# Two cross-attention layers in split fp32: the bias token's value added from its probabilities on VectorE instead of a 65-row product per head

## The reference, cut to what matters

```
x: (8, 100, 512)   ctx: (8, 361, 512)   H = 16 heads, K = 128
x = L0(x, ctx)                       # one attention without heads, residual
for i in (1, 2):                     # two layers with heads
    h  = layer_norm(x)
    qh = h @ wq + bq;  kh = ctx @ wk + bk;  vh = ctx @ wv + bv      # per head
    kh = concat([kh, bias_k]);  vh = concat([vh, bias_v])          # one more token
    w  = softmax(qh kh^T / sqrt(K));  c = w vh
    x  = x + c @ wo + bo
x = x + gelu(layer_norm(x) @ w_fc1 + b_fc1) @ w_fc2 + b_fc2
```

## Time and profile before

| | |
|---|---|
| median of 3 runs | 1837.41 us (1834.67 to 1837.85) |
| profiled execution, first to last instruction | 1836.4 us |
| TensorE busy | 1812.6 us, 99% |
| VectorE / ScalarE / GpSimd busy | 1122.9 / 805.7 / 761.4 us |
| mean granted TensorE clock | 0.998 |
| a layer pass | 389 us (129 to 518 us) in the first, 368 us (518 to 886 us) in the second |

### The profile page before, as it was taken

The page is one execution under the profiler, slowest core; times in us unless marked ns, Lnnn a source line. Parts: engine busy times, 40 slices in busy tenths (PEclk is TensorE's granted clock), DMA queues, the critical chain, the costliest instruction groups (busy, mean ns, idle before and its releaser), DMA issues.

```text
span 1836.4 us, 30800 instructions
## 1 busy us (share of the span) xinstructions
PE 1812.6 (99%) x11572; PEld 1776.0 (97%) x11572; DVE 1122.9 (61%) x2588; ACT 805.7 (44%) x1868; POOL 761.4 (41%) x624
## 2 busy tenths in 40 slices
PE   8999999999999999999999999999999999999999
PEld 5889999999999999999999999999999999999999
DVE  3667656565575565566687655566666556555565
ACT  3634334434444444344475443434435434434454
POOL 2674252352251453531478145252245252353244
PEclk9999999999999999999999999999999999999999
DMA  8933221121020121210373111111012020111122
GB/s 249 238 115 92 63 64 31 46 64 35 24 72 23 41 66 34 64 36 18 117 221 94 30 47 58 35 58 36 30 52 60 24 64 30 47 58 41 39 96 85
DMA packets 73590, 123.80 MB, mean 67 GB/s; under 512 B 13888, under 2 KB 25536, under 8 KB 73444
## 3 DMA queue, kind: packets, MB, share of 16 engines
q1 hardware_dynamic: 71140, 117.64, 21.7%
q10 hardware_dynamic: 2304, 4.20, 0.7%
HBM read 119.20 MB, written 2.61 MB: 66 GB/s over the span
## 4 chain that ended last, share of the span: by engine, by line
PE 90%; DVE 5%; DMA 2%; ACT 1%; issue 1%; POOL 0%; SPq 0%; DVEq 0%; ACTq 0%
PE psum L602 27%; PE psum L604 27%; PE psum L603 27%; PE psum L898 3%; PE psum L636 2%; DMA ctx_rows_in<-ctx_dram 1%; DVE xT L1568 1%; DMA key_stage_late<-head_w_dram 1%; PE psum L773 1%; PE psum L864 1%; PE psum L791 1%; PE psum L615 1%; PE psum L611 1%; DMA key_stage<-head_w_dram 0%; DVE h_lo L1367 0%
## 5 line engine op out<-in xcount | busy, mean ns | idle before, releaser
L484 POOL TENSOR_TENSOR wbuf_hi<-stage,zero_col 128x512 fp32r<-128x512 f32 x256 | 267.9, 1046 | 923.8 <-PE psum L604 545.3
L534 POOL TENSOR_TENSOR wbuf_lo<-stage,wbuf_hi 128x512 fp32r<-128x512 f32 x256 | 330.2, 1290 | 20.0
L602 PE MATMUL psum<-pT_hi,ctx_rows_hi 121*128 121x250 f32 (+3 forms) x1152 | 331.9, 288 | 1.2 <-DVE pT_lo L1363 1.2
L604 PE MATMUL psum<-pT_hi,ctx_rows_lo 121*128 121x250 f32 (+3 forms) x1152 | 332.3, 288 | 0.0
L603 PE MATMUL psum<-pT_lo,ctx_rows_hi 121*128 121x250 f32 (+3 forms) x1152 | 331.0, 287 | 0.0
L602 PE MATMUL psum<-ctxT_hi,a_hi 128*125 128x362 f32 (+1 forms) x832 | 280.4, 337 | 0.0
L604 PE MATMUL psum<-ctxT_hi,a_lo 128*125 128x362 f32 (+1 forms) x832 | 273.1, 328 | 0.0
L603 PE MATMUL psum<-ctxT_lo,a_hi 128*125 128x362 f32 (+1 forms) x832 | 272.7, 328 | 0.0
L1363 DVE TENSOR_TENSOR a_lo<-psum,a_hi 128x500 fp32r<-128x500 f32 (+2 forms) x288 | 146.0, 526 | 201.8 <-ACT a_hi L1019 200.9
L602 PE MATMUL psum<-a_hi,wbuf_hi 128*128 128x400 f32 x720 | 253.4, 352 | 0.0
L603 PE MATMUL psum<-a_lo,wbuf_hi 128*128 128x400 f32 x720 | 247.8, 344 | 0.0
(11 more groups left out here) (185 smaller groups left out, 3564.5 us busy)
## 6 DMA issues: line engine op xcount, KB each, us to landing
stage<-head_w_dram SPq DMA_DIRECT2D x256, 256.0 KB, 2.6
mlp_stage<-mlp_w_dram SPq DMA_DIRECT2D x32, 512.0 KB, 3.8
ctx_rows_in<-ctx_dram SPq DMA_DIRECT2D x12, 726.0 KB
ctxT_in<-ctxT_dram SPq DMA_DIRECT2D x12, 724.0 KB, 10.5
key_stage<-head_w_dram SPq DMA_DIRECT2D x22, 256.0 KB, 9.2
l0w<-l_w_dram ACTq DMA_DIRECT2D x16, 256.0 KB, 9.5
key_stage_late<-head_w_dram SPq DMA_DIRECT2D x10, 256.0 KB, 3.5
out_dram<-y_out SPq DMA_DIRECT2D x8, 200.0 KB, 2.6
```

The costliest lines, as they stand in the source:

```text
L484: return nc.gpsimd.tensor_tensor(out, in_, zero_col[0:in_.shape[0], :].broadcast_to(tuple(in_.shape)), ALU.add)
L534: nc.gpsimd.tensor_tensor(lo, held, hi.bitcast(F32), ALU.subtract).then_inc(stage_free, 1)
L602: pe.matmul(out, a_h, x_hi, start=start, stop=False)
L604: return pe.matmul(out, a_l, x_hi, start=False, stop=stop)
```

## The change

`dv3`, `pb3`, their clearing, copies and loads, and the thirteenth matmul of each value piece are gone. In their place:

- `probs_hi` on ScalarE issues, right after each of the 208 blocks' turned probabilities are copied, a DMA that writes column 0 of the normalised probabilities (125 elements of 4 bytes, one per partition) to DRAM.
- `exps` on ScalarE, which overwrites that buffer two blocks later, now also waits for that write to have landed (`p0_out`).
- `load_first_probs` on SP reads for each head 4 x 100 probabilities back, to all 128 partitions (200 KB, rows of 400 bytes, three buffers). It waits for the write of the head's last block, and for the add of the head three before (`p0_add`), and stands in SP's queue between the weight loads.
- `values_lo` on VectorE first adds `p0 * (bias_v - bv)` into the PSUM bank of v(h); `values_hi` on ScalarE waits for that, and VectorE then makes the low part as before.

```diff
+LAST_BLOCK_OF = [(UNIT_OF[h], NB - 1, UNITS[UNIT_OF[h]].index((h * L + L - 1) // BLK)) for h in range(H)]
+P0_READ_AT = [made_before_turn(*LAST_BLOCK_OF[h]) + WBUFS + STAGES for h in range(H)]
...
+            def load_first_probs(ph, h):
+                g = ph * H + h
+                s = ph * S_LAYER + S_AT[LAST_BLOCK_OF[h]]
+                sp.wait_ge(p0_out[s % 2], p0_written(s))
+                wait(sp, p0_add, g - P0_BUFS + 1)
+                sp.dma_start(p0_b[:, g % P0_BUFS, :, :], p0_d[ph, :, h * L:(h + 1) * L].partition_broadcast(P))\
+                  .then_inc(p0_ld[g % P0_BUFS], 16)
...
                     for i in range(early, W_LAYER):
+                        for h in range(H):
+                            if P0_READ_AT[h] == i:
+                                load_first_probs(ph, h)
                         load_weights(ph, i)
...
                 def values(h):
...
-                        mm3(out, chunk(hi, c), chunk(lo, c), a_hi[:, c, :, slot(h)], a_lo[:, c, :, slot(h)],
-                            start=(c == 0), stop=False)
-                    pe.wait_ge(dv_ld[h // 2 % 2], (ph * (H // 4) + h // 4 + 1) * 48)
-                    pe.matmul(out, dv3[:, h // 2 % 2, h % 2 * P:(h % 2 + 1) * P], pb3[:, :, slot(h)], start=False, stop=True)\
-                        .then_inc(y_mm, 1)
+                        mm = mm3(out, chunk(hi, c), chunk(lo, c), a_hi[:, c, :, slot(h)], a_lo[:, c, :, slot(h)],
+                                 start=(c == 0), stop=(c == DC - 1))
+                    mm.then_inc(y_mm, 1)
...
                 def values_hi(h):
+                    act.wait_ge(p0_add, ph * H + h + 1)
...
                 def exps(k, b, x):
...
+                    s = ph * S_LAYER + i
+                    if s >= 2:
+                        act.wait_ge(p0_out[s % 2], p0_written(s - 2))
...
                 def probs_hi(k, b, x):
...
                     copy(pT_hi[0:CH, :, pt_columns(k, x)], turned).then_inc(pt_hi, 1)
+                    s = ph * S_LAYER + S_AT[k, b, x]
+                    f0 = BLOCKS[UNITS[k][x]][0]
+                    act.dma_start(p0_d[ph, b, f0:f0 + rows], prob[0:rows, S_AT[k, b, x] % 2, 0:1]).then_inc(p0_out[s % 2], 16)
...
                 def values_lo(h):
+                    g = ph * H + h
+                    n = R_AT["v", h]
+                    dve.wait_ge(y_mm, ph * R_LAYER + n + 1)
+                    dve.wait_ge(p0_ld[g % P0_BUFS], g // P0_BUFS * 16 + 16)
+                    nc.vector.scalar_tensor_tensor(out=made("v", h), in0=p0_b[:, g % P0_BUFS, :, :],
+                                                   scalar=dv_cols[:, l * H + h:l * H + h + 1], in1=made("v", h),
+                                                   op0=ALU.mult, op1=ALU.add).then_inc(p0_add, 1)
```

More of the change, by code:

```diff
@@ L31 @@
 FULL_SCALE = float(D) ** -0.5
-BQ, BK, BV, BIAS_K = range(4)
+BQ, BK, BV, BIAS_K, BIAS_V = range(5)
 SCALE_COL, OFFSET_COL, RES_COL = range(3)
@@ L127, with made_before_turn @@
 MBUFS = 5
+def made_before_turn(k, b, x):
+    done = len(pieces("start"))
+    for kk, bb in STEPS:
+        after = {"a": len(pieces((kk, bb, "a"))), "m": len(pieces((kk, bb, "m"))), "b": len(pieces((kk, bb, "b")))}
+        if (kk, bb) == (k, b) and x == 0:
+            return done + after["a"] + after["m"]
+        if (kk, bb) == (k, b) and x < len(UNITS[k]) - 1:
+            return done + sum(after.values())
+        done += sum(after.values())
+        if (kk, bb) == (k, b):
+            return done
+    return done
 UNIT_OF = [next(k for k, unit in enumerate(UNITS) if sum(BLOCKS[unit[-1]]) >= (h + 1) * L) for h in range(H)]
+LAST_BLOCK_OF = [(UNIT_OF[h], NB - 1, UNITS[UNIT_OF[h]].index((h * L + L - 1) // BLK)) for h in range(H)]
+P0_READ_AT = [made_before_turn(*LAST_BLOCK_OF[h]) + WBUFS + STAGES for h in range(H)]
 def build(nc, xT_d, ctxT_d, ctx_d, l0w_d, alpha_d, head_w_d, cols_d, rows_d, norm_d, mlp_w_d, mlp_b_d, out_d):
@@ L219, in build @@
         prob = sb("prob", [P, 2, T])
[L220 to L221 removed]
+        p0_b = sb("p0_b", [P, P0_BUFS, NB, L])
+        sb("before_late", [P, NB * RING + 2 * 2 * P - P0_BUFS * N])
         with ExitStack() as before_aside:
@@ L415, in _ @@
             sp.dma_start(out_d[1], x0_out[:, :, :]).then_inc(landed, 16)
-            def load_bias_rows(ph, pair):
-                if pair >= 2:
-                    sp.wait_ge(y_mm, ph * R_LAYER + R_AT["v", 2 * pair - 3] + 1)
-                elif ph > 0:
-                    sp.wait_ge(y_mm, ph * R_LAYER)
-                else:
-                    sp.wait_ge(rows_clear, 2)
-                    sp.wait_ge(dv_out, 32)
-                at = ((ph % LAYERS) * H + 2 * pair) * P
-                for row, part in ((0, 0), (32, 0), (64, 1)):
-                    sp.dma_start(dv3[row:row + 1, pair % 2, :].bitcast(F32), dv_d[part:part + 1, at:at + 2 * P])\
-                      .then_inc(dv_ld[pair % 2], 16)
+            def load_first_probs(ph, h):
[5 more added lines that the diff above has]
+                  .then_inc(p0_ld[g % P0_BUFS], 16)
             for half in range(HALVES):
@@ L451, in _ @@
                                 load_late_key_weights(next(keys))
-                        if ORDER[i][0] == "v" and ORDER[i][1] % 2 == 0:
-                            load_bias_rows(ph, ORDER[i][1] // 2)
+                    for h in range(H):
+                        if P0_READ_AT[h] >= W_LAYER:
+                            load_first_probs(ph, h)
                     if l + 1 < LAYERS:
@@ L1263, in layer @@
                         exps(k, b + 1, 0)
-                        first_rows_hi(*before)
                         attended_hi(*before)
@@ L1282, in layer @@
                         run_pieces((k, b, "a"))
-                        if before is not None:
-                            first_rows_hi(*before)
                         exps(k, b, 1)
@@ L1672, in layer @@
                         normalise(k, b + 1, 0)
-                        first_rows_lo(*before)
                         attended_lo(*before)
@@ L1813 @@
         "head_w": np.concatenate([layer_w(1), layer_w(2)]).reshape(LAYERS * H * 4, P, D),
-        "cols": np.stack([both(n).reshape(LAYERS * H, P).T for n in ("bq", "bk", "bv", "bias_k")], 1),
-        "rows": np.stack([both(n).reshape(LAYERS * H, P) for n in ("bk", "bias_k", "bv", "bias_v")], 1)
-        .reshape(LAYERS * H, 2, 2, P),
+        "cols": np.stack([both(n).reshape(LAYERS * H, P).T for n in ("bq", "bk", "bv", "bias_k", "bias_v")], 1),
+        "rows": np.stack([both(n).reshape(LAYERS * H, P) for n in ("bk", "bias_k")], 1),
         "norm_p": np.stack([norm_cols("ln1_scale", "ln1_offset", "bo1"), norm_cols("ln2_scale", "ln2_offset", "bo2"),
```

68 lines of the change are left out of this document (20 added, 48 removed).

## The result

The changed kernel takes 2094.96 us (median of 4 runs, 2090.49 to 2097.22) against 1837.63 us of the kernel before beside it: 1.1402 times as long, 95% interval 1.1382 to 1.1423. I had forecast 1830.8 us, 0.36% faster.

A forecast was written before the change was run, and what follows sets the result against it. TensorE, busy 1812.6 of 1836.4 us, was taken as the bound. Terms -11.8 + 1.2 + 0.4 + 0.4 + 1.2 + 1.0 + 1.0 = -6.6 us gave 1829.8, a median of 1830.8 us; range 1825.4 to 1848, forecast's own 1827 to 1834.

The forecast's parts named there:

- What goes: On TensorE, 64 matmuls removed from the value pieces, 0.185 us each, all on the path: -11.8 us.
- The adds: 64 VectorE adds before ScalarE's copy delay o2, o7, o10 and the ends of passes: 1.2 + 0.4 + 0.4 us.
- ScalarE's issue: Issuing the DMA before unit 5's exponentials delays them 0 to 0.41 us; with the landing, 1.2 us in all.
- ScalarE's wait for the landing: Unit 5's exponentials wait 0 to 0.2 us for the block's write; with the issue, 1.2 us in all.
- 4.6 us: Write time beyond which every step would be held, costing tens of microseconds; 0.08 left for very late writes or unseen stalls.
- SP's loads: 64 loads of 200 KB on SP delay o13 to o15 at each pass's end: 1.0 us over four passes.
- X: How long one 200 KB load keeps the rings busy: 2.3 us taken, 0.9 to 6.4 possible; passes lose above 2.1.
- the rival of serial reads: Broadcast reads of one place queue up, X 6.4 us, each pass losing 4.3 us at its end: 1851.0 us, chance 0.17.
- v0 in the first pass: VectorE waits 4.3 us for head 0's load behind late key loads; 1.0 us lost once, bounds 0 and 6.
- all of it hides: Rival: issue hidden under the copy, adds fit, X below 2.1 us; -11.8 us, 1825.6 us, chance 0.15.
- ScalarE held: Rival: in unit 5 the issue doesn't overlap or writes land half a microsecond late; 6 us lost, 1835.6 us, chance 0.20.
- the mild rival: The ScalarE held case, which the read-modify-write rule was taken to give: 12 x 0.5 us, 1835.6 us, chance 0.20.

The follow-up runs named there:

- n1: n0 without the 64 adds, so only the 65-row products are gone (no writes, no loads): 1824.8 us, 0.993 of the kernel before.
- n0: a3 without the writes and the waits for them; products gone, adds kept: 1825.9 us, 0.9943 of the kernel before.
- b1: The changed kernel with its 4-byte pieces 64 bytes apart in another DRAM tensor and its loads reading rows from the weights: 1826.0 us, 0.9942 of the kernel before.
- m3: a3 with only 32 of each block's 4-byte pieces written, still side by side: 1841.7 us, 1.0027 of the kernel before.
- a5: The changed kernel writing one contiguous row per step instead of 4-byte pieces, SP writing each unit's last row: 1829.4 us, 0.996 of the kernel before.
- a2: The changed kernel without the writes and waits for them, its loads reading another small DRAM tensor: 1831.7 us, 0.9969 of the kernel before.
- m2: a3 with the 4-byte pieces written 512 bytes apart to another DRAM tensor: 1828.4 us, 0.9948 of the kernel before.
- m5: a3 with the 4-byte pieces written 64 bytes apart to another DRAM tensor: 1826.4 us, 0.9944 of the kernel before.
- a3: The changed kernel without the 64 broadcast loads; writes, ScalarE's waits and adds stay: 2042.1 us, 1.1105 of the kernel before.

## Why the prediction was wrong, by its own steps

**What goes: right.** -11.8 us forecast, -12.0 measured (n1, 9 to 16 by its interval).

**The adds: right within what can be told.** 0.63 us a piece taken, 638 ns measured:

```profile
L1602 DVE SCALAR_TENSOR_TENSOR psum<-p_b,dv_cols,psum 128x400 f32<-128x400 f32 x64 | 40.8, 638 | 54.7 <-PE psum L612 43.8 <-DMA p_b<-p_scratch 10.8
```

2.0 us forecast, 1.0 by n0 and n1. At a pass's end n0 needs 17.61 us from v12 to the last matmul of o15 and n1 17.28: 0.3 us a pass where I said 0.1.

**ScalarE's issue: my term was too high.** The issue takes 0.26 us, not 0.41, and it starts while the activation ahead of it still runs. In b1 the exponential of unit 5 is not later for it, so its price there is zero. The Trainium skill ("TensorE: Matmul & The Clock Gate", the section on the array's architectural detail) gives ScalarE a queue of 8 instructions, from which I had worked out that the issue would be hidden; the trace agrees.

**ScalarE's wait for the landing: the step that failed.** I took the landing of 125 pieces of 4 bytes from the 25 KB write of `s_scratch`, "from nothing to 0.2 us after 856.10", because it was the nearest row. It was near in what it shared (a write to DRAM, an engine's queue) and far in the one thing that decided: its pieces are whole rows, those of the new write are neighbours of 4 bytes. They land after 6.1 to 6.3 us with no other kind of transfer beside them, and after some 10 us in the row of step (4,1). I had said that beyond 4.6 us every step would be held, and left 0.08 for it; that was the case that came (128 of the 208 exponentials wait), and its size was wrong too: "tens of microseconds" against 269. The 4.6 us have no working in the prediction and no run confirms them: m3's writes land after 2.7 us and 44 exponentials already wait, 61.3 us in all. I had not costed three things in it. The slack is not everywhere 36 matmuls: in steps (2,1) and (4,1) the exponential follows its own step's copy, and TensorE wants its block after scores whose last matmul starts at 892.38, 3.8 us after the issue. The clock falls behind a long stall (0.50 in that row, 0.953 over the execution). And a slow write holds the other transfers.

**SP's loads: right in size.** I took X = 2.3 us, a landing of 3.8. In a5, where the load reads the rows from the same place, min/median/max:

```profile
DMA to landing us min/median/max: 3.0/3.5/4.2
```

X is 2.0 us, below my threshold of 2.1, and the pass's end loses nothing (17.55 us in a5, 17.61 in n0). A serial reading (6.4) is ruled out for these rows. But a2 warns: the same load from rows 4096 bytes apart in another tensor landed after a median of 7.8 us (5.1 to 12.1). There X is 6.3 us, and the pass's end loses 0.9 to 1.4 us (18.46 to 19.03 against 17.61), not the 4.2 my formula gives: so the rival of serial reads had a duration that does occur, its cause not shown, and an inflated price. One of my signs for it, a landing of `p_b` of 6 us or more, did come in the change (6.4 us), but a5 shows that the slow writes made it.

**v0 in the first pass: right place, too small.** a5 shows 4.5 us of VectorE's wait, as I had it (4.3), and TensorE held for 2.6 us where I took 1.0.

**The rivals.** With the pieces apart, b1 lands on "all of it hides", 1826.0 against 1825.6 us. "ScalarE held" was the right rival with a price for half a microsecond, and its sign, exponentials waiting for `p_scratch`, is what the profile shows. My forecast's two forms also don't quite agree: -4 to -9 us is 1828 to 1833 us, and I wrote 1827 to 1834.

**The rule I quoted.** The Trainium skill ("DMA: Bandwidth & Descriptors", Specifications) says that transfers below 512 B are read, modified and written back. I took from it only the mild rival, half a microsecond a write. The runs agree in part: m2, m5 and b1 write pieces of 4 bytes without a visible loss, so size alone costs little; side by side they cost 216 us (a3 against n0). Whether a read-modify-write is the cause no run shows.

## What to carry to other kernels

A column of one element per partition, written side by side to DRAM, is to be feared for the distance between its pieces: put them at least 64 bytes apart, or turn the column into one row first, on chip, and write that. When a new transfer is priced from an old one, compare the shape of the pieces on the side that is written, not the bytes; and when a threshold is a factor of two away from the nearest row, and everything is held behind it, the rival deserves its full price. Where such a slow write has to stay, more buffers in front of the waiting engine give back most (222 of 269 us here); the other transfers stay slow, which costs where the path waits for one.

## What was unexpected of the hardware

- 125 pieces of 4 bytes side by side in DRAM: 6.3 us from issue until the waiting exponential starts, with no traffic but a second such write (100 pieces quite alone: 6.1 us). The same 64 bytes apart: landed within 2.7 us. Into one row of SBUF: a loss of some 5 us over the whole kernel.
- While they are under way other transfers slow down: weights from 2.6 to 5.2 us (median), 2048-byte packets from 110 to 249 ns on average. Whether the pieces wait in the DRAM or in the DMA engines no run here tells.
- The broadcast load landed in 3.5 us from rows 6400 bytes apart (3.4 from 6144 bytes, in the weights) and in 7.8 us from rows 4096 bytes apart. The tensors differed too, so the distance is a guess.
- ScalarE issues a DMA in 0.26 us while its activation runs; in the rows of unit 5 of b1 that delays nothing.
